# A two-layer graph network: running sums along streams of chunks instead of sums kept by tile

## The chip, the cores and the metric

The kernel runs on one core of a Trainium2 chip (trn2). The metric is the device time of one execution, in microseconds. Engines: TensorE (PE, its weight loads PEld), VectorE (DVE), ScalarE (ACT), GpSimd (POOL) and SyncE (SP), which here only issues DMAs.

## The reference

The graph has N = 1250 nodes, E = 20000 edges (sorted by destination), features of D = 768 floats and 34 relations.

```python
def gatv2(x, src, dst, Ws, bs, Wd, bd, attn):
    fs = (x @ Ws + bs).reshape(-1, H, D)
    fd = (x @ Wd + bd).reshape(-1, H, D)
    e = leaky_relu(fs[src] + fd[dst], 0.2)
    logits = einsum('ehd,hd->eh', e, attn)
    m = segment_max(logits, dst)
    ex = exp(logits - m[dst])
    alpha = ex / segment_sum(ex, dst)[dst]
    return elu(segment_sum(alpha[:, :, None] * fs[src], dst))
h = layer_norm(gatv2(x, ..., attn1) + x)        # 8 heads
h = layer_norm(gatv2(h, ..., attno))            # 1 head
# layer 1: mean over the edges of each (relation, node), 34 products,
# a root product, then a normalised sum over edges
h1 = einsum('rni,rio->no', mean, W_rel) + h @ W_root + b_rgcn
xw = h1 @ W_gcn
out = segment_sum(xw[src] * (dinv[src] * dinv[dst])[:, None], dst) + xw * dinv**2 + b_gcn
```

## The kernel before, in words

Nodes are ranked by their number of incoming edges and stand in ten tiles of 128 partitions. A chunk is four edges (S = 4) of one node; a group is one chunk of each of the 128 nodes of one tile. A tile needs as many groups as its richest node has chunks; a table `tile_of_group` says which tile each group belongs to. For these inputs there are 47 groups; loops run turns of U = 4 groups, so 12 turns, 48 groups. Buffers have four slots, one for each group of a turn.

The stages, in order, with all engines meeting between them:

- First stage: sorting of the edges and the two first projections fs and fd. VectorE builds `tile_of_group` there (lines 714 to 722).
- First attention, 8 heads (`attention`). GpSimd (`gather_edges`, lines 811 to 874) issues four indirect DMAs per group, one row `fs[src]` of 3104 B for each partition (`rows_of`, line 805), and one that reads a group's 4 edge records (line 828); it works out which of them are real (lines 830, 834). Rows are fetched two groups ahead (ROWS_AHEAD = 2), once TensorE has read the slot's old rows. The fd rows of all ten tiles are gathered once (`fdt`, line 1015; nine of the ten behind the first two groups' rows). VectorE and TensorE add fs and fd, ScalarE sums the logits of three edges head by head (line 1038), VectorE does the fourth's, the softmax with a running maximum, and the weighting of three edges (line 1194); TensorE adds the four rows (`pA`, line 1102); VectorE adds this into `acc` of the tile (line 1165).
- Then layer norm and two projections (`settle_first`).
- Second attention, 1 head (`attention_single`, `gather_rows`, lines 910 to 924). For group u, TensorE first runs `add` for group u + 2 (it waits for those rows), then the share products `pA` of group u (16 matmuls, line 1330, which free the slot: `summed`), then the product with the old `acc` (line 1335); ScalarE copies the result back into `acc` (line 1283). VectorE also counts the edges of each relation.
- Then layer norm and the root product (`settle_last`).
- Relation products: per list of 128 (relation, node) pairs, a gather, six transposes, 36 matmuls, a scatter; VectorE cuts the operands in two parts (line 2203 and those behind it).
- Edge sum: GpSimd fetches four rows of the products per group (line 805 again); VectorE works out each edge's weight from the counts by relation (lines 2399 to 2408) and sums two edges of the four, TensorE the other two (`pR`, line 2335), and VectorE adds them to `acc` (line 2383). Beside it a matrix of edge counts between nodes is built (ScalarE line 2304, TensorE `pC`, VectorE line 2375), already transposed.
- The product with W_gcn, then the final product with the count matrix, and the output.

Accumulators (`acc`, `den`, `cntge`, `counts`) live in SBUF by tile; each engine reads the tile number of the turn's groups from `tile_of_group` (`sum_tiles`, line 773). Results are brought from rank order to node order by indirect DMAs.

The order of the work is written out by hand: each engine's instruction list is one queue in order, and GpSimd's indirect DMAs are issued from its own list. What waits at the head of a list holds all behind it.

Of the kernel before, what the change touches and what calls it, by code (L numbers as in the profile page):

```python
# [5 lines left out]
ALU = mybir.AluOpType  # L6
ACT = mybir.ActivationFunctionType
X = mybir.AxisListType.X
# [10 lines left out]
W = D + HEADS  # L19
HALF = D // 2  # L20
# [3 lines left out]
TBACK = 2  # L24
PACK = 6
EROWS = 10016
PROJ_COLS = 100
TG = 5120
# [4 lines left out]
MARKS = 4  # L33
BIG = 1e30
# [35 lines left out]
def gnn_kernel(nc, io, out):  # L70
    ctx = ExitStack()
    with ctx:
# [19 lines left out]
        groups_d = dram("groups_d", (MAX_TURNS * U + U - 1, P, S * 2), I32)  # L92
        by_rank_d = dram("by_rank_d", (NP, 4), I32)
        tile_of_group_d = dram("tile_of_group_d", (TG,), I32)
# [8 lines left out]
        perm_d = dram("perm_d", (NP,), I32)  # L103
# [10 lines left out]
        C_TURNS, C_RANKS, C_PAIRS, C_MORE, C_REL = 0, 2, 3, 4, 8  # L114
        tile_of_group = sb("tile_of_group", [P, TG], I32)
        perm = sb("perm", [P, NT + 1], I32)
        permc = sb("permc", [P, NT + 1], I32)
        degr = sb("degr", [P, NT + 1], F32)
        relbase = sb("relbase", [P, RELS + 1], F32)
        recs = sb("recs", [EP, EC, 2], I32)  # L120
        first_row = sb("first_row", [P, NT + 1], I32)
# [26 lines left out]
        kept_d = dram("kept_d", (P, NT, D), F32)  # L148
# [50 lines left out]

        def w_view(w):  # L200
            return w.rearrange("(c p) n -> p c n", p=P)
# [27 lines left out]
        with stage() as st:  # L229
            lower = sb("lower", [P, P], F32, st)  # L230
            mrow = sb("mrow", [P, 1792], F32, st)
            arow = sb("arow", [P, DA], F32, st)
            gidx = sb("gidx", [P, TG // P, PACK], F32, st)
# [20 lines left out]
            junk = sb("junk", [P, 1792], F32, st)  # L254
# [4 lines left out]
            kmax = sb("kmax", [P, NT], F32, st)  # L259
            kmaxi = sb("kmaxi", [P, NT], I32, st)  # L260
            gend = sb("gend", [P, NT], F32, st)
            small = sb("small", [P, 4], F32, st)
            tog = sb("tog", [P, TG // P, PACK], F32, st)
            packed = sb("packed", [P, TG // P], F32, st)
            togi = sb("togi", [P, TG // P], I32, st)
# [4 lines left out]
             unsorted_sum, deg_sb, deg_out, deg_in, prefixes, ranks, by_rank_out, by_rank_in, maxima, tog_ready,  # L270
             tog_out, tog_in, zero_ready, clear, degr_ready, recs_ready, recs_out, ctl_ok) = sems(
                 st, "const_built", "dve_step", "edges_in", "prev_in", "onehots", "degrees",
                 "backs", "unsorted_sum", "deg_sb", "deg_out", "deg_in", "prefixes", "ranks",
                 "by_rank_out", "by_rank_in", "maxima", "tog_ready", "tog_out", "tog_in",
                 "zero_ready", "clear", "degr_ready", "recs_ready", "recs_out", "ctl_ok")
            CONSTS = 15
# [26 lines left out]
            v_in, dve3, dve3b, copied, posted, none_ok, none_out = sems(  # L303
                st, "v_in", "dve3", "dve3b", "copied", "posted", "none_ok", "none_out")
# [22 lines left out]

            def x_rows(a, i, b, rows, behind=0):
                if isinstance(i, int):
                    at = (2 * i + b) * P + behind  # L330
                    return a[at:at + rows, :]
                return a[ds(i * (2 * P) + (b * P + behind), P), :]

            with nc.Block() as block:
                @block.sync
                def _(sp):
# [22 lines left out]
                    sp.wait_ge(zero_ready, 1)  # L359
                    sp.dma_start(by_dst_d.rearrange("(p f) c -> p (f c)", p=P), zeros[:]).then_inc(clear, 16)  # L360
# [23 lines left out]
                    sp.wait_ge(tog_ready, 1)  # L384
                    sp.dma_start(tile_of_group_d.rearrange("(p c) -> p c", p=P), togi[:]).then_inc(tog_out, 16)
                    sp.wait_ge(tog_out, 16)
                    sp.dma_start(tile_of_group[0:1, :], tile_of_group_d.unsqueeze(0)).then_inc(tog_in, 16)
# [10 lines left out]
                    for s in h_out + f_out[0] + f_out[1]:  # L398
                        sp.wait_ge(s, 16 * 5)
                    sp.wait_ge(none_out, 16)  # L400
                    sp.wait_ge(recs_out, 16)
                    sp.wait_ge(tog_in, 16)

                @block.gpsimd
                def _(pool):
# [2227 lines left out]
```

## Time and profile before

| | us |
|---|---|
| time, three runs | 3326.93, 3327.62, 3331.6 (median 3327.62) |
| span of the profiled execution | 3343.9 |
| first attention, edge loop | about 249 to 907 |
| second attention, edge loop | about 1110 to 1584 |
| relation products | about 1758 to 2741 |
| edge sum | about 2751 to 3140 |
| final product and output | about 3226 to 3344 |

The profile shows one execution; only its span is given for it. "Busy" is the time in which an engine's instructions ran; an arrow names what ended the idle time before an instruction. PEclk is the granted TensorE clock (1.00 is 2.4 GHz, 0.50 is 1.2 GHz).

### The profile page before, as it was taken

To read this page: it belongs to the slowest core of one execution; us is meant where nothing else is said; L and a number is where in the kernel's file an instruction comes from. 1 tells how busy PE (TensorE), PEld (TensorE's weight loads), DVE (VectorE), ACT (ScalarE), POOL (GpSimd) and SP (SyncE) were. 2 spreads that over 40 slices of the span, in tenths; PEclk is the share of its full clock that TensorE was granted. 3 is DMA by queue.
4 is the path that set the end of the run, shared out by engine and by line. 5 is a ranking of instruction groups with operands and counts; after the bars stand their busy time and mean duration, and the time that the engine had idled before them with its cause. 6 is when DMAs were issued, how large, how long until landed. Compare 5 with 4: busy or idle time off the path is not lost. (4 is left out here: it accounts for less than half of the span.)

```text
span 3343.9 us, 59649 instructions
## 1 busy us (share of the span) xinstructions
PE 2854.4 (85%) x13556; PEld 2139.5 (64%) x13557; DVE 2290.3 (68%) x4351; ACT 1702.4 (51%) x5372; POOL 1620.6 (48%) x2067
## 2 busy tenths in 40 slices
PE   5885888888789799998668999999999976777799
PEld 3442454454455455554348999999999974555598
DVE  6535889889767788887565555555555447888743
ACT  0004889899722133332545566555665566777300
POOL 4666566565446555554114545544544445555201
PEclk9897999999999899999789999999999998999899
DMA  4235344444511555555228777777776747666412
GB/s 141 84 81 159 121 135 126 124 134 124 170 46 44 157 167 170 171 170 175 89 95 263 243 242 245 242 237 237 247 241 219 222 144 230 203 210 208 119 34 65
DMA packets 175008, 546.00 MB, mean 163 GB/s; under 512 B 55331, under 2 KB 56343, under 8 KB 174723
## 3 DMA queue, kind: packets, MB, share of 16 engines
q0 software_dynamic: 82000, 370.33, 35.3%
q1 hardware_dynamic: 70596, 122.50, 11.8%
q10 hardware_dynamic: 22304, 52.11, 5.4%
q14 instruction: 86, 0.70, 0.1%
q8 instruction: 22, 0.36, 0.0%
HBM read 461.31 MB, written 83.81 MB: 163 GB/s over the span
## 5 line engine op out<-in xcount | busy, mean ns | idle before, releaser
L2189 PE MATMUL pO<-wh,gT 128*128 128x384 f32 x3264 | 867.1, 339 | 17.6 <-ACT gT L2140 15.6
L805 POOL DMA_INDIRECT row<-fs_d,rec x400 | 455.9, 1140 | 389.6 <-PE pA L1330 157.5
L2189 PEld LDWEIGHTS pO<-wh,gT 128*128 128x128 f32 x3264 | 594.4, 189 | 26.4 <-ACT gT L2140 23.0
L2189 PE MATMUL pO<-wl,gT 128*128 128x384 f32 x1632 | 547.5, 335 | 0.0
L2203 DVE TENSOR_SCALAR cntge<-pT 128x768 int32<-128x768 int32 x137 | 131.2, 958 | 427.2 <-ACT gT L2140 223.1
L1038 ACT ACTIVATE sj<-sj 128x96 f32<-128x96 f32 x1176 | 312.9, 268 | 78.7 <-DVE sj L1155 78.5
L2189 PEld LDWEIGHTS pO<-wl,gT 128*128 128x128 f32 x1632 | 308.3, 189 | 0.0
L2140 ACT ACTIVATE gT<-cntge 128x256 fp32r<-128x256 f32 x822 | 292.9, 410 | 28.1 <-DVE cntge L2206 4.0
L805 POOL DMA_INDIRECT row<-y_d,rec x200 | 204.1, 1020 | 171.6 <-PE pR L2335 113.5
L1077 PE MATMUL pS<-row,ident 128*128 128x384 f32 x400 | 176.2, 524 | 128.3 <-DVE sj L1155 80.9
L2335 PE MATMUL pR<-row,share 128*128 128x384 f32 x384 | 165.7, 582 | 120.6 <-issue 65.0
L170 PE MATMUL pO<-wt,hT 128*128 128x384 f32 (+1 forms) x720 | 242.9, 497 | 19.8 <-issue 8.0
L1330 PE MATMUL pA<-row,share 128*128 128x384 f32 x768 | 255.6, 486 | 1.0 <-ACT share L1296 1.0
L1102 PE MATMUL pA<-row,ident 128*128 128x384 f32 x768 | 255.5, 486 | 0.0
L208 POOL DMA_INDIRECT marked_d<-marks,recc x160 | 201.7, 1261 | 65.4 <-issue 54.2
L2065 POOL DMA_INDIRECT g<-hr_d,gindex x138 | 167.7, 1215 | 121.6 <-POOL keys L2062 60.8
L1038 ACT ACTIVATION_READ_ACCUMULATOR sj<-sj 128x1 f32 x1176 | 220.4, 187 | 0.5 <-issue 0.2
L170 PEld LDWEIGHTS pO<-wt,hT 128*128 128x128 f32 (+1 forms) x720 | 137.7, 193 | 118.6 <-issue 31.5
L1330 PEld LDWEIGHTS pA<-row,share 128*128 128x128 f32 x768 | 145.8, 190 | 103.1 <-issue 1.9
L1102 PEld LDWEIGHTS pA<-row,ident 128*128 128x128 f32 x768 | 145.9, 190 | 101.8
L1077 PEld LDWEIGHTS pS<-row,ident 128*128 128x128 f32 x400 | 76.0, 200 | 202.3 <-DVE sj L1155 109.3
L2129 ACT ACTIVATE acc<-startrow,after 128x1279 bf16<-128x1279 f16 (+1 forms) x139 | 188.1, 1353 | 27.9 <-DMA startrow<-seen_d 27.9
(386 smaller groups left out, 5983.8 us busy)
## 6 DMA issues: line engine op xcount, KB each, us to landing
fdt<-in_L_gnn_W_rel_dram SPq DMA_DIRECT2D x170, 384.0 KB
startrow<-seen_d ACTq DMA_DIRECT2D x141, 320.0 KB
raw<-in_L_gnn_W_rel_dram SPq DMA_DIRECT2D x34, 384.0 KB
row<-fs_d,rec POOLq DMA_INDIRECT x400
kept_d<-fdt SPq DMA_DIRECT2D x10, 384.0 KB
kept<-kept_d SPq DMA_DIRECT2D x10, 384.0 KB
fs_d<-of SPq DMA_DIRECT2D x9, 388.0 KB
fd_d<-of SPq DMA_DIRECT2D x9, 388.0 KB
```

Of the source, the lines that this page charges most:

```text
L170: last = pe.matmul(dst[0:rows, q, 0:HALF], rows_t[:, c * P:c * P + rows], w[:, c, lo:up], start=c == 0, stop=c == KC - 1)
L208: pool.indirect_dma_start(marked_d[k], bass.IndirectOffsetOnAxis(ap=keys, axis=0), marks[0:EP], None)\
L805: pool.indirect_dma_start(b["row"][u][:, j, :].bitcast(words), None, table, bass.IndirectOffsetOnAxis(ap=b["rec"][u][:, 2 * j + field:2 * ...
L1038: last = act.activation(of_head, of_head, ACT.Copy, accum_out=dots[off % U][:, j, h:h + 1])
L1077: pe.matmul(pS[j][:, q, 0:HALF], ident[:], row[off % U][:, S // 2 + j, lo:up], start=True, stop=False)
L1102: last = pe.matmul(pA[:, q, 0:HALF], share, row[u][:, j, lo:up], start=j == 0, stop=j == S - 1)
L1330: last = pe.matmul(pA[u % 2][:, q, 0:HALF], share[u % 2][:, 1 + j, :], row[u][:, j, lo:up], start=j == 0, stop=False)
L2065: pool.indirect_dma_start(g[:, b, :], None, hr_d, bass.IndirectOffsetOnAxis(ap=gindex[b][:], axis=0))\
L2129: act.activation(sign[:, 0:COUNT[b]], seen_row[b][:, 0:COUNT[b]], ACT.Sign, bias=half, scale=-1.0, accum_out=total[b][:]).then_inc(total_o ...
L2140: act.activation(gT[:, c].bitcast(F32R), cut[:, :, c * P:(c + 1) * P], ACT.Copy).then_inc(gT_ok.sem, 1)
L2189: last = pe.matmul(pO[:, q, 0:HALF], gT[:, c, half, :].bitcast(F32R), w[:, c, lo:up].bitcast(F32R), start=c == 0 and k == 0, stop=c == KC ...
L2335: last = pe.matmul(pR[:, q, 0:HALF], share[u % 2][:, k, :], b["row"][u][:, BY_DVE + k, lo:up], start=k == 0, stop=k == S - BY_DVE - 1)
```

## The change

The 1250 nodes are dealt to 128 streams, one for each partition, by rank in turns forward and backward, so that the streams are nearly equally long. A partition walks the chunks of its nine or ten nodes one after another; a group is now the next chunk of every stream. For these inputs the longest stream has 44 chunks: 11 turns, 44 groups, in each of the three edge loops.

Partitions of one group are now at different nodes, so nothing can be kept by tile. Each group reads its own fd row for every partition with a fifth indirect DMA (`own_of`; not in the edge sum); sums run on from group to group in four slots (`sum`), with a flag or a factor `keep` that is zero at a node's first chunk; and each group's running row is scattered to DRAM (`sums_out`, two groups behind), where the rows that are not a node's last lie out of bounds and are skipped. Before a group's record slot is reloaded, GpSimd copies the scatter's target (`keep_target`). In the first attention the fetch of rows (fd row first) stands ahead of the record and of the scatter; in the second attention and in the edge sum the scatter and the copy of the target stand ahead of the fetch.

```diff
+        def keep_target(pool, b, i, off):
+
+            u = off % U
+            sum_free(pool, b, i, off)
+            pool.sem_inc(b["posted"], 1)
+            pool.tensor_copy(b["to"][u][:], word(b, u, R_OUT)).then_inc(b["to_ok"][u], 1)
+        def sums_out(pool, b, i, off, table, done):
+
+            u = off % U
+            for s in done:
+                s.wait(pool, i, off)
+            target_wait(pool, b, i, off)
+            pool.sem_inc(b["posted"], 1)
+            pool.indirect_dma_start(table, bass.IndirectOffsetOnAxis(ap=b["to"][u][:], axis=0), b["sum"][u][:], None,
+                                    bounds_check=NP - 1, oob_is_err=False).then_inc(b["sum_out"][u], 16)
...
+            def fetch(i, off):
+                u = off % U
+                pool.wait_ge(b["edges_only"][u], i * 16 + 16 * (off // U + 1))
+                used.wait(pool, i, off - U)
+                pool.sem_inc(b["posted"], 1)
+                own_of(pool, b, u, own)
+                rows_of(pool, b, u, table, 0, F32)
...
             with pool.Fori(0, turns) as i:
                 for u in range(U):
+                    fetch(i, u + ROWS_AHEAD)
+                    w = u + U - 1
                     rows_wait(pool, b, i, u - 1)
+                    own_wait(pool, b, i, u - 1)
+                    pool.wait_ge(b["saved"][w % U], i * 16 + 16 * (w // U))
+                    pool.wait_ge(b["info_in"][w % U], i * 16 + 16 * (w // U + 1))
                     pool.sem_inc(b["posted"], 1)
+                    record(w % U)
+                    sums_out(pool, b, i, u - LAG, out_table, done)
+                    keep_target(pool, b, i, u)
+                    edges_only(i, w)
+            for k in range(LAG, 0, -1):
+                sums_out(pool, b, turns, -k, out_table, done)
...
+            def fetch(i, off):
+                u = off % U
+                rec_wait(pool, b, i, off)
+                for used in readers:
+                    used.wait(pool, i, off - U)
+                pool.sem_inc(b["posted"], 1)
+                if own is not None:
+                    own_of(pool, b, u, own)
                 rows_of(pool, b, u, table, field, words)
...
                 for u in range(U):
-                    w = u + ROWS_AHEAD
-                    pool.wait_ge(b["rec_in"][w % U], i * 16 + 16 * (w // U + 1))
-                    for used in readers:
-                        used.wait(pool, i, w - U)
-                    pool.sem_inc(b["posted"], 1)
-                    rows_of(pool, b, w % U, table, field, words)
+                    sums_out(pool, b, i, u - LAG, out_table, done)
+                    keep_target(pool, b, i, u)
+                    fetch(i, u + ROWS_AHEAD)
...
+                        def keep(i, off):
+                            whole.wait(act, i, off)
+                            sum_free(act, b, i, off)
+                            act.activation(split(total[off % U][:, 0:D]), halves(pA[off % 2]), ACT.Copy).then_inc(kept.sem, 1)
```

A first-stage loop over blocks of 64 groups writes what each group of each stream needs (16 words: edges or weights, row, node, flags), with 22 steps on VectorE, in place of the ten steps over `tile_of_group`:

```diff
+                    with dve.Fori(0, blocks) as k:
+                        w = Steps(dve, dve_step, k * BLOCK_STEPS + v.base)
+                        w.wait()
+                        w.link(dve.tensor_tensor(begun[:], over(grow[:], 2, shape), over(chunk_from[:], 1, shape), ALU.is_ge))
+                        for f in range(5):
+                            w.link(dve.tensor_tensor(part[:], begun[:], over(rise[:, f, :], 1, shape), ALU.mult))
+                            w.link(dve.tensor_reduce(now[:, f, :], part[:], X, ALU.add))
...
+                        w.mark(dve.scalar_tensor_tensor(out=word(R_OUT), in0=is_last, scalar=float(NP), in1=node,
                                                         op0=ALU.mult, op1=ALU.add))
...
+                        w.mark(dve.tensor_scalar(fword(R_KEEP), is_first, -1.0, 1.0, ALU.mult, ALU.add))
+                        w.mark(dve.tensor_scalar(grow[:], grow[:], float(BLOCK), None, ALU.add))
+                        w.wait()
+                        dve.sem_inc(block_ready, 1)
+                        assert w.n == BLOCK_STEPS, w.n
```

The edge sum takes its weights from these words; they are worked out during the relation products, once for each relation, ahead of the next relation's weights, and the count matrix is kept as running rows of 16-bit integers that are no longer transposed by `pC`:

```diff
+                    def weigh(i, b):
+
+                        v = Steps(dve, weigh_step, i * 6 + (3 * b + 1))
+                        v.wait()
+                        sh = [P, 2 * S, RELS]
+                        at = ds(i * (4 * S) + b * (2 * S), 2 * S) if not isinstance(i, int) else slice((2 * i + b) * 2 * S, (2 * i + b + 1) * 2 * S)
+                        row = ds(i * 4 + b * 2, 2) if not isinstance(i, int) else slice((2 * i + b) * 2, (2 * i + b + 1) * 2)
+                        of_group = crow[:, row, :].unsqueeze(2).to_broadcast([P, 2, S, RELS])
+                        v.link(dve.tensor_tensor(crel[:], over(reld[:, at], 2, sh), over(relid[:], 1, sh), ALU.is_equal))
+                        v.link(dve.tensor_tensor(crel[:].rearrange("p (g s) r -> p g s r", g=2),
+                                                 crel[:].rearrange("p (g s) r -> p g s r", g=2), of_group, ALU.mult))
+                        v.mark(dve.tensor_reduce(cweight[:].rearrange("p g s -> p (g s)")[:, at], crel[:], X, ALU.add))
+                        assert v.n == 3
...
                         cut_rows(end * PAIR, -1)
+                        weigh(i, b)
                         if more:
                             cut_weights(i, b + 1, range(KC // 2))
...
-                            weight_ok.wait(dve, i, u)
+                            compare(i, u + 1)
                             rows_wait(dve, b, i, u)
-                            into = of_acc(tile)
+                            summed.wait(dve, i, u)
+                            used.wait(dve, i, u - 1)
+                            sum_free(dve, b, i, u)
+                            dve.scalar_tensor_tensor(out=split(total[u][:, 0:D]), in0=split(total[(u - 1) % U][:, 0:D]),
+                                                     scalar=word(b, u, R_KEEP, F32), in1=halves(pR),
+                                                     op0=ALU.mult, op1=ALU.add).then_inc(added.sem, 1)
                             for j in range(BY_DVE):
...
+                                dve.scalar_tensor_tensor(out=total[u][:, 0:D], in0=row[u][:, j, :],
+                                                         scalar=word(b, u, R_WEIGHT + j, F32), in1=total[u][:, 0:D],
+                                                         op0=ALU.mult, op1=ALU.add).then_inc(used.sem, 1)
+                            joined.wait(dve, i, u)
+                            counted.wait(dve, i, u - 1)
+                            dve.scalar_tensor_tensor(out=count[u], in0=count[(u - 1) % U], scalar=word(b, u, R_KEEP, F32),
+                                                     in1=pC[u % 2][:].rearrange("p a f -> p (a f)")[:, 0:NP],
+                                                     op0=ALU.mult, op1=ALU.add).then_inc(counted.sem, 1)
```

The later stages load and store plain rows in node order with DMAs of SyncE instead of indirect ones. The product with W_gcn first adds the edge sums that it loads to the root part (ten additions). The final stage loads the counts tile by tile, widens them on VectorE and transposes them on TensorE, ten transposes for each tile:

```diff
+                        def turn(t):
+                            pe.wait_ge(wide_ok, t + 1)
+                            if t > 0:
+                                pe.wait_ge(ch_ok, t)
+                            for c in range(NT):
+                                last = pe.transpose(pW[:, c // 4, (c % 4) * P:(c % 4 + 1) * P], wide[t % 2][:, c * P:(c + 1) * P], ident[:])
+                            last.then_inc(turned, 1)
```

The big memsets of `acc`, the gather of `fdt`, and all reads of `tile_of_group` are gone.

## Rows read from the trace of the kernel before

**Rows 1.** Busy time by engine in five stretches: the three edge loops, root product, last product
```profile
core 0: us, PE busy (x) PEld busy (x) DVE busy (x) ACT busy (x) POOL busy (x), PEclk, DMA share, GB/s
300.00:907.00 607.00, 523.08 (x1546) 295.00 (x1544) 538.52 (x1002) 541.75 (x3124) 359.62 (x472) 0.98 0.44 131
1130.00:1584.00 454.00, 439.36 (x1337) 251.90 (x1336) 383.78 (x1047) 136.54 (x345) 233.40 (x184) 1.00 0.58 170
1587.00:1758.00 171.00, 114.06 (x332) 61.54 (x332) 101.51 (x203) 83.21 (x106) 26.04 (x51) 0.80 0.29 97
2760.00:3140.00 380.00, 274.22 (x2304) 194.16 (x2304) 324.10 (x532) 275.52 (x288) 201.04 (x197) 0.90 0.67 206
3226.00:3344.00 118.00, 106.14 (x600) 105.82 (x600) 43.26 (x42) 0.00 (x0) 12.30 (x10) 0.95 0.22 70
```

**Rows 2.** First attention, VectorE: the line run once for each group
```profile
L1165 DVE TENSOR_TENSOR acc<-pA,scaled x49: 946/947/958, 306.6 to 905.1; 128x768 f32 x49
```

**Rows 3.** First attention, VectorE timeline: the first instruction of two groups, start and length
```profile
...
613.40 0.19 DVE L1175 TENSOR_TENSOR lg<-dots,lin 128x32 f32<-128x32 f32 x1 [0.73 <-ACT sj L1038]
...
625.46 0.22 DVE L1175 TENSOR_TENSOR lg<-dots,lin 128x32 f32<-128x32 f32 x1
```

**Rows 4.** First attention, GpSimd timeline of its first groups
```profile
...
290.26 0.95 POOL L1015 DMA_INDIRECT fdt<-fd_d,permc  x1 [0.30 <-issue]
...
300.99 0.20 POOL L825 COPY now<-left 128x2 f32 x1
...
309.58 1.43 POOL L805 DMA_INDIRECT row<-fs_d,rec  x1 [0.30 <-issue]
```

**Rows 5.** First attention, GpSimd by line: busy us, mean ns, idle before
```profile
L805 POOL DMA_INDIRECT row<-fs_d,rec x182 | 186.7, 1026 | 165.9 <-PE pA L1102 111.5 <-issue 42.0 <-POOL rec L834 12.4
```

**Rows 6.** First attention, TensorE's share sums: durations, first and last start
```profile
L1102 PE MATMUL pA<-row,ident x768: 486/486/486, 309.9 to 904.3; 128*128 128x384 f32 x192
```

**Rows 7.** Second attention, ScalarE: the line run once for each group
```profile
L1283 ACT ACTIVATE acc<-pA x49: 784/810/813, 1130.8 to 1582.7; 128x768 f32 x49
```

**Rows 8.** Second attention, timeline of one group and the fetch behind it
```profile
...
1300.20 5.32 PE L1330 MATMUL pA<-row,share 128*128 128x384 f32 x16
...
1305.36 1.45 PE L1335 MATMUL pA<-acc,share 128*128 x4
1306.34 1.41 POOL L805 DMA_INDIRECT row<-fs_d,rec  x1 [3.44 <-PE pA L1330]
...
1307.08 0.81 ACT L1283 ACTIVATE acc<-pA 128x768 f32 x1 [2.15 <-PE pA L1335]
...
1311.12 0.95 POOL L805 DMA_INDIRECT row<-fs_d,rec  x1 [0.30 <-issue]
...
1315.88 0.91 PE L1312 MATMUL pS<-row,ident 128*128 128x384 f32 x2
```

**Rows 9.** Second attention, waits: us in total, times, longest
```profile
PE pS L1312 <- DMA row<-fs_d,rec: 7.4, 13, 1.2
```

**Rows 10.** Second attention, GpSimd by line
```profile
L805 POOL DMA_INDIRECT row<-fs_d,rec x182 | 231.5, 1272 | 192.5 <-PE pA L1330 149.5 <-issue 43.0
```

**Rows 11.** The whole span, GpSimd by line: a scatter of full rows
```profile
L1761 POOL DMA_INDIRECT hr_d<-ht,sindex x10 | 9.8, 979 | 35.2 <-ACT ht L1805 35.2
```

**Rows 12.** Edge sum, VectorE: the line run once for each group
```profile
L2383 DVE TENSOR_TENSOR acc<-acc,pR x49: 933/942/955, 2767.4 to 3136.2; 128x768 f32 x49
```

**Rows 13.** Edge sum, GpSimd by line
```profile
L805 POOL DMA_INDIRECT row<-y_d,rec x190 | 194.5, 1024 | 164.4 <-PE pR L2335 113.5 <-issue 45.4 <-DVE acc L2421 4.6
```

**Rows 14.** First stage, VectorE timeline
```profile
...
109.15 5.00 DVE L716 SCALAR_TENSOR_TENSOR tog<-gidx,gend,tog 128x240 f32<-128x240 f32 x10
```

**Rows 15.** First stage, TensorE timeline
```profile
...
119.95 0.88 PE L163 MATMUL pT<-ident,ht 128*128 128x128 f32 x6
...
137.67 2.92 PE L170 MATMUL pO<-wt,hT 128*128 128x384 f32 x4 [4.78 <-DVEq L754]
```

**Rows 16.** Relation products, VectorE by line
```profile
L2203 DVE TENSOR_SCALAR cntge<-pT 128x768 int32<-128x768 int32 x137 | 131.2, 958 | 427.2 <-ACT gT L2140 223.1 <-PE pT L163 203.2 <-issue 0.9
```

More of the change, by code:

```diff
@@ L23 @@
 U = 4
-TBACK = 2
-PACK = 6
 EROWS = 10016
 PROJ_COLS = 100
-TG = 5120
+BLOCK = 64
+GROUPS = 5120
+WORDS = 16
+R_ROW, R_NODE, R_LEFT, R_FLAG, R_OUT, R_KEEP, R_NODEF = range(8, 15)
+R_WEIGHT = S * 2
 MAX_TURNS = (E // S + NT) // U + 1
@@ L832, in edges_only @@
-            def edges_only(u):
-                pool.tensor_tensor(b["rec"][u][:], b["rec"][u][:], b["edge"][u][:], ALU.mult).then_inc(b["edges_only"][u], 16)
-            ahead = sum_tiles(pool, 0, U - 1, 0)
-            for u in range(U - 1):
-                record(pre, u, ahead[u])
-                pre.wait()
-            for u in range(ROWS_AHEAD):
-                pool.wait_ge(b["rec_in"][u], 16)
-                edges_only(u)
-                pool.wait_ge(b["edges_only"][u], 16)
-                rows_of(pool, b, u, table, 0, F32)
@@ new lines, in fetch @@
+            def fetch(i, off):
+                u = off % U
+                pool.wait_ge(b["edges_only"][u], i * 16 + 16 * (off // U + 1))
+                used.wait(pool, i, off - U)
+                pool.sem_inc(b["posted"], 1)
+                own_of(pool, b, u, own)
+                rows_of(pool, b, u, table, 0, F32)
+            for u in range(U - 1):
+                pool.wait_ge(b["info_in"][u], 16)
+                record(u)
+            for off in range(ROWS_AHEAD):
+                edges_only(0, off)
+                fetch(0, off)
@@ L996, in attention @@
                 lin_ok = Signal(st, "lin_ok", 1, U, U)
-                top_ok = Signal(st, "top_ok", 1, U, U)
                 den_ok = Signal(st, "den_ok", 1, U, U)
-                row = b["row"]
-                def fdt_row(tile):
-                    return fdt[:, tile, :] if isinstance(tile, int) else fdt[:, ds(tile, 1), :].rearrange("p o f -> p (o f)")
+                row, own, total = b["row"], b["own"], b["sum"]
                 with nc.Block() as block:
@@ L1100, in _ @@
                                     for q, lo, up in HB:
-                                        share = ident[:] if heads > 1 else shares[:, j, :]
-                                        last = pe.matmul(pA[:, q, 0:HALF], share, row[u][:, j, lo:up],
+                                        last = pe.matmul(pA[:, q, 0:HALF], ident[:], row[u][:, j, lo:up],
                                                          start=j == 0, stop=j == S - 1)
@@ L2378, in add @@
-                    def add(i, off, tile):
-                        summed.wait(dve, i, off)
-                        used.wait(dve, i, off)
-                        into = split(of_acc(tile))
-                        dve.tensor_tensor(into, into, halves(pR), ALU.add).then_inc(added.sem, 1)
+                    for u in range(U - LAG, U):
+                        pre.mark(dve.memset(total[u][:], 0.0))
+                    dve.wait_ge(node_ok, 1)
+                    pre.link(dve.tensor_copy(of_node[:], node[:]))
```

1114 lines of the change are left out of this document (590 added, 524 removed).

## The prediction

> **What bounds the kernel now.** I read the busy time by stretch first, then in each edge loop the line that runs once per group, then the timeline of one group. Three loops take 1441 of the 3343.9 us of span, and no engine is the bound in all of them. First attention [rows 1]: VectorE 539 and ScalarE 542 us busy of 607. 48 intervals of line 1165 take 905.1 - 306.6 = 598.5 us [rows 2], so 12.47 us a group; inside a turn two groups stand 12.06 apart [rows 3], and the rest is lost at turn boundaries. Second attention: TensorE 439 of 454 us at full clock; 48 intervals of line 1283 take 451.9 us [rows 7], 9.41 a group. Edge sum: VectorE 324 of 380, 48 intervals in 368.8 us [rows 12], 7.68 a group. In the last product TensorE works 106 of 118 us.
>
> The reader should see a second limit in the second attention [rows 8]. TensorE's sums of a group end at 1305.52; that frees a row slot; GpSimd's four fetches start at 1306.34 and the last at 1311.12; the matmul that needs them starts at 1315.88, 4.8 after that, and in 13 of the 46 groups it is seen waiting for its rows, by up to 1.2 [rows 9]. Then come 2.7 us of `pS` (8 half matmuls at 5.32/16 = 0.33) and 5.32 of `pA`, which free the next slot but one: 10.36 + 2.7 + 5.3 = 18.4 us for two groups, 9.2 for one. The loop from a slot's release to its next release is as long as TensorE's own work. Whatever is put into it is paid in full, half of it per group.
>
> **The change part by part.** From the inputs the longest stream has 44 chunks, where the tiles needed 47: 44 groups instead of 48 in each loop. Everything else is price.
>
> *First attention.* VectorE does about the same per group (a copy goes, the running sum is written to a new slot) but reads no tile numbers at turn boundaries: 12.0. GpSimd gets more. Its unhindered turn of one group is now 309.58 + 1.43 - 300.99 = 10.0 us [rows 4]. Three small operations and their hand-overs go (-1.5), the own fd row comes (0.95 to 1.03 + 0.30 = 1.3 [rows 5]), the scatter (0.98 + 0.30 [rows 11]), the copy of the target (0.4) and a little waiting for the record that it has just asked for and now masks at once, not one group later: 11.5, and with the slower GpSimd operations that stand beside VectorE up to 13. Nothing hides it, but it is not in a short loop: rows are asked for two groups ahead. Two engines at nearly 12.0 give 12.3 (bounds 11.8 and 13.1): 44 x 12.3 = 541, minus 598.5 = -57. At the start, nine fd gathers (1.25 each, until 291.2 [rows 4]) stood between the second group's rows and the third's, and the first share sum waited for those until 309.9 [rows 6]; they go, with the large memset, against two fd rows and masks in order: -20. At the end the last scatter has to land: +3. Sum -74 (-95 to -30).
>
> *Second attention.* The scatter waits for the sum of its group to be copied by ScalarE, and stands ahead of the fetch. From the slot's release: 1.3 to the end of the old sum's product, 0.3 and 0.8 for ScalarE's copy (ends 1307.89 [rows 8]), 0.8 until GpSimd starts (as at 1306.34), 0.98 for the scatter [rows 11], 0.6 for the copy of the target and the hand-over, 0.3, then the own fd row, 1.27 + 0.30 [rows 10]: the first row is asked for 6.6 us after the release, now 0.8. That is +5.8 (5.2 if the fd row takes 0.95). Behind it nothing changes. 18.4 + 5.8 = 24.2 for two groups, 12.1 for one; with GpSimd's operations quicker beside a less busy VectorE (0.95 against 1.27 on average, five of them) 11.3. I take 11.85, nearer to the upper end since the sample group's fetches were themselves under the mean: 44 x 11.85 = 521, minus 452 = +69. The fill is +3 (two fd rows), the last scatter +5. Sum +77. Bounds: if the loop did not bind, 44 x 9.41 = 414 and -38 + 8 = -30; with 12.6, +110.
>
> *Edge sum.* VectorE loses the four operations that make weights; at 324/48 = 6.75 now it falls to about 6.3. GpSimd: five indirect DMAs of 1.02 [rows 13] with 0.30 between them, the copy of the target and two hand-overs, 7.3 (7.0 if all are quick, 8.0 if each hand-over takes 0.8). Here the release of a slot and its next use lie four groups apart, so the order scatter-then-fetch costs nothing but the engine's time. 44 x 7.3 = 321, minus 369 = -48; start -3 (no zeroing of the counts), last scatter +4. Sum -47 (-65 to -10).
>
> *The rest.* First stage: ten steps over 240 elements (5.00 us [rows 14]) and seven small ones, 7.4 in all, give way to a block with eleven steps over 640 elements, by their size 0.8 each, and eleven small ones: 13 to 14. TensorE waits for VectorE there [rows 15], so +6 (+3 to +10). Layer norm after the first attention: plain loads of the same rows, +2. Root product: 48 small gathers on GpSimd, which is busy 26 of 171 us [rows 1], hide; the chain of relation counts moves ahead of the sums: +3 (-5 to +11). Relation products: 34 times three VectorE operations over 272 elements, some 1.2 us each time; VectorE stands idle 427 us ahead of its first cut alone [rows 16], but at a change of relation they come before the new weights: +3 (0 to +20). Product with W_gcn: the ten additions hide behind TensorE except the first, +3. Last product: 100 transposes of 0.88/6 = 0.147 us [rows 15] on the engine that is the bound, 14.7, and a first widening; one output DMA less on GpSimd's way: +15. Sum +32.
>
> Total: -74 + 77 - 47 + 32 = -12 us. This is worked against the profiled execution, 3343.9 us of span, 16.3 us (0.5%) above the median; scaling changes nothing that counts. 3327.6 - 12 = 3316.
>
> Scatters of which most rows are dropped do not occur in the trace before. The nearest is a scatter of full rows at 0.98 [rows 11]; skipped rows may make it cheaper (0.5) or the bound test dearer (2). In the second attention 0.5 less is -11, 1 more is +22; in the edge sum as much times two. I take 0.98 and keep the ends for the range.
>
> **A rule weighed.** In the second attention TensorE works 97% of the time and the granted clock is 1.00; in the edge sum it works 72% with gaps for which it waits and the granted clock is 0.90 [rows 1]. After the change the second attention has TensorE busy 9.1 of 11.85 us, 77%, with one long wait for rows in each group. The Trainium skill, "TensorE: Matmul & The Clock Gate", section "HAM oscillation — how this bites in real kernels", describes a kernel whose matmuls are shorter than its waits for data and which therefore falls back to the lower clock every time. By that rule the wait would also slow the matmuls; by the clock of 1.00 it would not, and my sum has it so. The trace agrees as far as the edge sum shows.
>
> **The rivals.**
>
> 1. *The loop does not bind* (something in my chain runs beside the rest). Second attention -30 instead of +77: 3209. Against it: the 13 waits for rows in the loop before, and that each link is an order written in the code. Chance 0.08.
>
> 2. *The clock falls in the second attention* (the other side). 9.4 us of matmuls (1.45 + 2.7 + 5.3) lie in the loop over two groups. At the edge sum's 0.90 they take 1.0 more, 0.5 per group, +23; at the root product's 0.80 [rows 1] 2.35, 1.2 per group, +52. In the middle +37: 3353. It decides as soon as a group takes over 12.3. For it: 23% of waiting. Against: the first attention, with 14% of waiting, keeps 0.98. Chance 0.22.
>
> 3. *GpSimd is the bound and slow*: 13.0 per group in the first attention (+31), 7.8 in the edge sum (+22), since each of its operations is exposed to VectorE's: 3369. For it: 1.27 us per fetch in the second attention against 1.03 in the first [rows 5, 10]. Against: with GpSimd as the bound, VectorE has pauses in which it runs free. Chance 0.14. [...]
>
> 4. *The trade is better than I think*: first attention at 11.9 per group and scatters at 0.5 us: -18 - 11 - 21 = -50, 3266. It lies in my range's lower part. For it: most rows of a scatter are skipped. Against: so far a scatter costs what a fetch does [rows 11]. Chance 0.10.
>
> **How the numbers follow.** The forecast, 3316 (its own range 3290 to 3340), has 0.46; the rivals 0.08, 0.22, 0.14 and 0.10. Below 3250 lies rival 1, above 3380 a tail of rivals 2 and 3; the range is 3250 to 3380. A measurement of this kernel tells 0.2% (6.7 us) from no change. Faster (below 3321): 0.6 of the forecast's 0.46, rivals 1 and 4, little of 2: 0.47. Same (3321 to 3334): 0.22 of 0.46 and 0.05: 0.15. Slower: 0.38.
>
> **What would show it.** In the changed kernel's trace: 45 executions of the per-group lines; 12.3 us a group in the first attention, 11.85 in the second with GpSimd's scatter ahead of the fetch and TensorE waiting for rows about 2.5 us in every group at clock 1.00; 7.3 in the edge sum with GpSimd busy or handing over all the time; a first share sum some 40 us after the start of the first attention, not 60. I am wrong if the second attention takes under 10.5 a group (rival 1), if its clock is 0.90 or less (rival 2), or if GpSimd's own turn in the other loops is over 12.8 or 7.7 us (rival 3).

## The result and the profile after

The changed kernel takes 3429.34 us (median of 4 runs, 3421.63 to 3433.7) against 3329.61 for the kernel before (median of 4, 3326.93 to 3334.01): slower, ratio 1.0295, 95% interval 1.028 to 1.0309. The forecast was 3316 in a range of 3250 to 3380. The profiled execution of the changed kernel has a span of 3419.9 us.

Each line that runs once per group, in the three edge loops of the changed kernel (durations, first and last start); they answer to [rows 2], [rows 7] and, with one execution less since it counts in the same turn, [rows 12]:

```profile
L1261 DVE TENSOR_TENSOR sum<-pA,scaled x45: 946/957/959, 292.2 to 879.6; 128x768 f32<-128x768 f32 x45
L1365 ACT ACTIVATE sum<-pA x45: 787/810/811, 1112.8 to 1681.9; 128x768 f32<-128x768 f32 x45
L2522 DVE SCALAR_TENSOR_TENSOR sum<-sum,rec,pC x44: 1534/1543/1543, 2878.9 to 3188.9; 128x1280 int16<-128x1280 int16 x44
```

So a group takes 587.4/44 = 13.35 us in the first attention (12.47 before, 12.3 forecast), 569.1/44 = 12.93 in the second (9.41, 11.85), and 310.0/43 = 7.21 in the edge sum (7.68, 7.3). The two attentions by engine (columns as in [rows 1]):

```profile
300.00:880.00 580.00, 487.50 (x1392) 274.75 (x1390) 480.59 (x853) 488.02 (x2796) 405.55 (x427) 0.94 0.52 159
1130.00:1682.00 552.00, 439.63 (x1206) 248.99 (x1204) 339.86 (x873) 118.86 (x306) 301.23 (x295) 0.90 0.54 166
```

In the second attention no engine is busy for even 80% of the time, and the clock has fallen from 1.00 to 0.90. Laid out by milestones, the two profiled executions differ by 76 us of span:

| stretch | change forecast | measured |
|---|---|---|
| start to the first attention's first sum | -14 | -14.4 |
| first attention, 44 intervals against 48 | -57 | -11.1 |
| to the second attention's first copy | +8 | +7.5 |
| second attention, 44 against 48 | +69 | +117.2 |
| to the first relation product | +8 | +14.7 |
| relation products | +3 | -16.1 |
| to the last count of the edge sum | -51 | -47.0 |
| to the first product with W_gcn | +7 | +14.8 |
| the last two products and the output | +15 | +10.6 |

The medians differ by 100, not 76, because the profiled execution of the kernel before was 14 us above its median and that of the changed kernel 9 below. One stretch that varies between executions is the relation products: in the profiles of the changed kernel and of the eleven variants below, none of which touches them, they take 959 to 974 us, against 975 in the one profile of the kernel before. Of the -16, most is therefore not put down to the change; a few us may belong to it.

One group of the second attention in the changed kernel, its timeline (start us, us):

```profile
...
1307.07 1.45 PE L1414 MATMUL pA<-sum,share 128*128 128x384 f32 x4
...
1308.36 0.81 PE L1393 MATMUL pS<-row,ident 128*128 128x384 f32 x2
...
1308.63 0.81 ACT L1365 ACTIVATE sum<-pA 128x768 f32<-128x768 f32 x1 [13.22 <-PE pA L1414]
...
1310.47 1.65 POOL L896 DMA_INDIRECT second_d<-sum,to  x1 [6.82 <-issue]
...
1310.94 5.32 PE L1409 MATMUL pA<-row,share 128*128 128x384 f32 x16
...
1312.11 0.93 POOL L887 COPY to<-rec 128x1 int32<-128x1 int32 x1
...
1313.20 1.01 POOL L847 DMA_INDIRECT own<-fd_d,rec  x1 [0.16 <-issue]
...
1318.26 0.95 POOL L843 DMA_INDIRECT row<-fs_d,rec  x1 [0.30 <-issue]
...
1323.61 1.64 PE L1393 MATMUL pS<-row,ident 128*128 128x384 f32 x2 [6.06 <-DMA row<-fs_d,rec]
...
1328.64 1.78 PE L1409 MATMUL pA<-row,share 128*128 128x384 f32 x5
```

This is the chain the prediction laid out, link by link: end of the sum, ScalarE's copy, scatter, copy of the target, fd row, four rows, the wait, `pS`. The reader should see three links that are longer in this group than I had them: the scatter 1.65 (I had 0.98), the last request to its use 5.35 (4.8), and `pS`, which needs 5.0 us (1323.61 to 1328.64) and not 2.7, since it runs at the lower clock just after TensorE stood idle for 6.06 (granted clock 0.50 from 1323.6 to 1328.2).

The groups come in pairs. `pS` of one group starts right behind the sum of the group before and takes 2.6 us (1308.36 to 1310.94, granted clock 1.00); `pS` of the next waits for its rows and is slow. From 1130 to 1682, 22 groups are of the first kind, with `pS` at 2.58 on average, and 21 of the second, with a wait of 5.3 (112.2 us in all) and `pS` at 4.78, between 4.1 and 5.3. The forecast had the same waiting spread evenly, 2.5 in every group.

GpSimd in the first attention of the changed kernel, by line (busy us, mean ns, idle before; window 300 to 870, 43 groups):

```profile
L843 POOL DMA_INDIRECT row<-fs_d,rec x169 | 196.6, 1163 | 51.7 <-issue 51.7
L847 POOL DMA_INDIRECT own<-fd_d,rec x42 | 50.4, 1199 | 42.2 <-POOL rec L922 29.9 <-issue 10.7 <-PE pA L1197 1.5
L896 POOL DMA_INDIRECT first_d<-sum,to x44 | 47.4, 1077 | 14.1 <-issue 14.1
L909 POOL DMA_INDIRECT rec<-by_dst_d,rec x43 | 41.9, 974 | 13.1 <-issue 13.1
L918 POOL TENSOR_SCALAR edge<-slot,rec 128x8 int32<-128x8 f32 x43 | 37.0, 861 | 35.4 <-issue 35.2
L887 POOL COPY to<-rec 128x1 int32<-128x1 int32 x43 | 18.6, 433 | 0.0
L922 POOL TENSOR_TENSOR rec<-rec,edge 128x8 int32<-128x8 int32 x43 | 14.6, 340 | 8.0 <-POOL edge L918 8.0
```

Busy 406.5 and idle 164.5 make 571 us, the whole window, and of the idle time only 1.5 us ends on another engine (`pA`). The rest is GpSimd handing over to itself or, by my reading of the 35.2 us before the mask (L918), waiting for the record that it has just asked for: in e3 and e5 below, which ask for it earlier, the mask waits 0.0 and 1.0 us in all. 571/43 = 13.3: the period of the loop is GpSimd's list.

### The profile page after: what moved, and what is told of

Same layout as the page of the kernel before. It is cut to its first block and busy times, and to the rows that moved or that the text cites. A ratio compares the mean times of both kernels' runs of the same rounds, so it can differ in the third digit from the quotient of the medians.

```text
span 3419.9 us, 54141 instructions
## 1 busy us (share of the span) xinstructions
PE 2814.0 (82%) x11992; PEld 2066.6 (60%) x11993; DVE 2190.5 (64%) x3987; ACT 1615.7 (47%) x5047; POOL 1773.2 (52%) x2181
## 5 line engine op out<-in xcount | busy, mean ns | idle before, releaser
L843 POOL DMA_INDIRECT row<-fs_d,rec x368 | 421.4, 1145 | 112.4 <-issue 111.5
L2328 DVE TENSOR_SCALAR cut<-pT 128x768 int32<-128x768 int32 x137 | 131.0, 956 | 362.0 <-ACT gT L2263 186.5
L1138 ACT ACTIVATE sj<-sj 128x96 f32<-128x96 f32 x1080 | 287.4, 267 | 76.9 <-DVE sj L1250 76.8
L2263 ACT ACTIVATE gT<-cut 128x256 fp32r<-128x256 f32 x822 | 291.4, 410 | 27.5 <-DVE cut L2331 4.3
L1176 PE MATMUL pS<-row,ident 128*128 128x384 f32 x368 | 172.5, 554 | 127.5 <-DMA row<-fs_d,rec 126.1
L1365 ACT ACTIVATE sum<-pA 128x768 f32<-128x768 f32 x45 | 36.4, 810 | 441.3 <-PE pA L1414 441.3
L1441 DVE TENSOR_TENSOR leak<-row,own 128x768 f32<-128x768 f32 x135 | 121.3, 954 | 182.8 <-DMA row<-fs_d,rec 182.8
L1409 PE MATMUL pA<-row,share 128*128 128x384 f32 x704 | 235.6, 488 | 0.0
L1197 PE MATMUL pA<-row,ident 128*128 128x384 f32 x704 | 234.2, 486 | 0.0
L1393 PE MATMUL pS<-row,ident 128*128 128x384 f32 x184 | 104.8, 661 | 139.1 <-DMA row<-fs_d,rec 139.1
L2252 ACT ACTIVATE sign<-startrow,after 128x1279 bf16<-128x1279 f16 (+1 forms) x139 | 188.4, 1356 | 28.5 <-DMA startrow<-seen_d 26.1
```

Of the source, the lines that this page charges most:

```text
L843: pool.indirect_dma_start(b["row"][u][:, j, :].bitcast(words), None, table, bass.IndirectOffsetOnAxis(ap=b["rec"][u][:, 2 * j + field:2 * ...
L1138: last = act.activation(of_head, of_head, ACT.Copy, accum_out=dots[off % U][:, j, h:h + 1])
L1176: pe.matmul(pS[j][:, q, 0:HALF], ident[:], row[off % U][:, S // 2 + j, lo:up], start=True, stop=False)
L1197: last = pe.matmul(pA[:, q, 0:HALF], ident[:], row[u][:, j, lo:up], start=j == 0, stop=j == S - 1)
L1409: last = pe.matmul(pA[u % 2][:, q, 0:HALF], share[u % 2][:, 1 + j, :], row[u][:, j, lo:up], start=j == 0, stop=False)
L2252: act.activation(sign[:, 0:COUNT[b]], seen_row[b][:, 0:COUNT[b]], ACT.Sign, bias=half, scale=-1.0, accum_out=total[b][:]).then_inc(total_o ...
```

## The experiments

All are variants of the changed kernel (3429 us), timed against the kernel before in turns on the same chip. "Period" is the spacing of the per-group lines above.

**e1 and e2: fetch ahead of the scatter.**

```diff
                 for u in range(U):
+                    fetch(i, u + ROWS_AHEAD)
                     sums_out(pool, b, i, u - LAG, out_table, done)
                     keep_target(pool, b, i, u)
-                    fetch(i, u + ROWS_AHEAD)
```

e1 in both stages that use this loop, e2 in the second attention alone.

> The changed kernel (3429 us, 12.93 us a group in the second attention, 7.2 in the edge sum) with the fetch of rows put ahead of the scatter and the copy of the target in both the second attention and the edge sum. Theory: the second attention is set by a loop over two groups (release of a slot, sum, copy, scatter, copy of the target, fetch, landing, sums); the order alone put about 5.8 us into it. Without it 18.4 + 1.6 for the own fd row and about 1 for a longer burst = 21 us for two groups, or GpSimd's own 9.7 us: 9.9 to 10.5 a group, 44 x -2.7 = -120; the edge sum is bound by GpSimd's total and stays at 7.2; the last fetches go out sooner, so each stage drains up to 5 us sooner. 3290 to 3315 us. Rival: the order costs nothing and the second attention is slow for its fifth DMA, its traffic and its clock: 3420 to 3430.

> Fetch ahead of the scatter in the second attention only; the edge sum keeps the scatter first. Theory: nearly all of the gain of the kernel with both, since the edge sum's slot comes back only after four groups: within 8 us of it, so 3295 to 3320. Rival: the edge sum's order costs as much per group as the second attention's: 50 us or more above the kernel with both.

Measured: e1 3330.27 us, ratio to the kernel before 0.9995 (0.9982 to 1.0009); e2 3327.53, 0.9985 (0.9976 to 0.9995). The line of e1:

```profile
L1365 ACT ACTIVATE sum<-pA x45: 785/811/814, 1116.3 to 1579.8; 128x768 f32<-128x768 f32 x45
```

463.5/44 = 10.53 us a group, at a clock of 0.99. The order alone is worth 44 x 2.4 = 106 us in this stage, as much as the 99 by which the change is slower. Some 0.95 of the 2.4 is the clock: its waits for rows are shorter (1.6 us on average, 28 of them from 1130 to 1575), and `pS` takes 2.73 on average, against (4.78 + 2.58)/2 = 3.68. The times miss the upper bounds of 3315 and 3320 by 15 and 8 us. A group gained 2.4 and not 2.7, which is 13 us, and the stage does not drain sooner, as the theory had it: from the last copy to the first instruction of the next stage it is 13.0 us in e1 (1579.8 to 1592.8) and 13.5 in the changed kernel (1681.9 to 1695.4). In the edge sum the period is 7.13 with fetch first and 7.15 with scatter first: there the order is free, as predicted.

**e9: the scatter three groups behind**, still ahead of the fetch.

```diff
-        LAG = 2
+        LAG = 3
```

> The changed kernel with one constant changed: sums are scattered three groups behind instead of two (in all three loops), the scatter still ahead of the fetch. Theory: what the second attention pays for is the wait of the scatter for a sum that was only just finished; three groups behind, the scatter and the copy of the target run before the slot is released, and the order is harmless: 10.3 to 11.0 a group, like fetch-first (10.53), 3325 to 3345 us. Rival: it is the GpSimd time in front of the fetch (scatter 1.2, copy 0.4, hand-overs) that costs, wait or no wait: 1.6 to 2.4 us stay in the loop of two groups, 11.4 to 12.0 a group, 3360 to 3395 us. First attention and edge sum: no change.

Measured: 3334.0 us, 1.0016 (1.0001 to 1.0031), period 10.51 in the second attention (45 executions of L1365, first and last start at 1120.6 and 1583.2). In the first attention the period is 13.50, as in e10, which leaves that stage alone, and in the edge sum 7.12: no change, as expected.

So it is not GpSimd's time for the scatter that costs. It is that the scatter, at the head of the list, waits for a sum which is finished only after the slot is released, and holds the fetch behind it. When the sum is one group older, scatter and copy run while GpSimd has nothing to do.

**e7: no fd row in the second attention.** The fd rows are a constant there, so that part of the computation is left out.

```diff
-                    own_of(pool, b, u, own)
+                    pool.sem_inc(b["own_in"][u], 16)
```

> The changed kernel without the fifth DMA of the second attention: the fd rows are a constant there (so this part of the computation is left out), the scatter stays ahead of the fetch. Theory of the loop over two groups: 1.3 to 1.4 us go from a chain of 25.9, and up to 1.5 of the transfer, which was a quarter longer: 12.93 down to 11.5 to 12.3 a group, -28 to -63: 3366 to 3401 us. Rival (GpSimd's total is the bound, 9.3 us of it): a full 1.4 per group, and rival (the scatter alone is the cause): under 10 us in all, above 3419.

Measured: 3383.63 us, 1.0158 (1.0129 to 1.0186), 46 us below the changed kernel; period 11.95, clock 0.93. One DMA of 1.09 + 0.30 us less takes 0.98 from the period, a good two thirds of it. Half, 0.70, is its place in a chain of two groups. A further 0.31 is the clock: after its wait `pS` takes 4.15 on average here, against 4.78. Together that is 1.01. A loop bound by GpSimd's total would give 1.4.

**e3, e4 and e5: GpSimd's list in the first attention.** e4 puts the fd row behind the four rows. e3 asks for the next record ahead of the fetch; e5 also copies the target there:

```diff
                 for u in range(U):
-                    fetch(i, u + ROWS_AHEAD)
                     w = u + U - 1
...
                     record(w % U)
+                    keep_target(pool, b, i, u)      # e5 only
+                    fetch(i, u + ROWS_AHEAD)
                     sums_out(pool, b, i, u - LAG, out_table, done)
-                    keep_target(pool, b, i, u)      # e5 only
                     edges_only(i, w)
```

> The changed kernel with one thing moved in the first attention: GpSimd asks for the next edge records before it fetches rows, not after, so that they have landed when it masks them. Theory: GpSimd's own list is the bound there (13.35 us a group = four rows 4.65 + fd row 1.2 + record 0.97 + scatter 1.08 + copy and masks 1.6 + hand-overs and waits 3.8); 0.8 us of waiting for the record and some of the 0.9 before the fetch go: 12.0 to 12.6 a group, 44 times -0.75 to -1.35 = -33 to -60: 3370 to 3396 us. Rival: the loop is bound by the transfers of the rows (TensorE waits for them 92 us there): no change, 3422 to 3436.

> The changed kernel with the fd row fetched after the four source rows in the first attention instead of before. Theory (GpSimd's list is the bound): the same operations in the same list, no change beyond 0.2%: 3422 to 3436. Rival: the fd row is what VectorE and TensorE wait for first, and last in the list it lands 1.3 us x 4 later for the first addition: up to +0.5 us a group, 3440 to 3451.

> As e3 (record asked for ahead of the fetch in the first attention), and the copy of the scatter's target also ahead of the fetch, so that SyncE's load of the next record words, which waits for that copy, is done a group earlier. Base: the changed kernel, 3429 us. Theory: GpSimd's own list is the bound; e3 failed because its record request then waited 2.8 us for that load. Now neither wait is left: per group five fetches 7.2, record 1.3, scatter 1.4, copy and masks 1.5, hand-overs 0.6: 12.0 to 12.5 instead of 13.35, -37 to -60: 3369 to 3392 us. Rival (the rows' transfers are the bound): 3422 to 3445.

Measured: e4 3431.04 us, 1.0312 (1.029 to 1.0334), period 13.35, no change: the fd row's place, first or last, does nothing. e3 3445.52, 1.0353 (1.0333 to 1.0373), period 13.61: worse, against both theories. Its waits (total, times, longest) say why:

```profile
POOL rec L909 <- DMA rec<-groups_d: 100.4, 37, 3.8
```

The record's request needs words that SyncE loads only once GpSimd has copied the slot's old target, and that copy now stood only 3.7 us ahead of the request (586.92 and 590.60 in one group), which waited 2.8 us for the load. I moved an operation past its queue and did not ask what else it waits for. e5 moves the copy too: 3377.2 us, 1.0146 (1.0113 to 1.0179), 52 below the changed kernel:

```profile
L1261 DVE TENSOR_TENSOR sum<-pA,scaled x45: 945/948/958, 293.5 to 829.4; 128x768 f32<-128x768 f32 x45
```

12.18 a group instead of 13.35. The same transfers and the same number of operations on every engine, but GpSimd's list (window 300 to 820) holds 9.2 us of work and 2.95 of idle time per group instead of 9.45 and 3.83: GpSimd was the bound.

**e10: a memset of 768 floats per group in the edge sum's list.**

> The changed kernel with a memset of 768 floats, which no one needs, put into GpSimd's list of the edge sum, once per group ahead of the fetch. Theory: GpSimd's list is the bound there (7.2 us a group); the memset (0.73 us for 768 in this kernel's trace, 0.2 of hand-over) is paid in full: +0.9 to 1.0 a group, +37 to +46: 3466 to 3475 us. Rival (VectorE, ScalarE or the transfers at 240 GB/s are the bound): less than +15, below 3444 us.

Measured: 3485.61 us, 1.0464 (1.0437 to 1.0491), 56 more than the changed kernel and 10 above the expected range. GpSimd by line in the edge sum (window 2900 to 3200):

```profile
L843 POOL DMA_INDIRECT row<-y_d,rec x142 | 147.9, 1041 | 64.5 <-issue 29.9 <-POOL spare L1031 26.4 <-DVE sum L2522 6.4
```

The memset takes 0.79 (28.3 us in 36) and the fetch waits 26.4/36 = 0.73 for it, not 0.2: 1.5 us, of which 1.12 arrive in the period (8.33 against 7.21). The missing 0.4 is no slack: the first row no longer has its own hand-over of some 0.3, and rows take 1.04 on average against 1.09. Without the memset the list is already full, with 248.1 us busy and 58.6 idle in the 305 from 2880 to 3185, and under 7 of these idle us end on another engine or on a load of SyncE. The edge sum is bound by GpSimd.

**e8: twelve turns instead of eleven.**

```diff
-  small[:, 0:1], most[:], float(U - 1), None, ALU.add
+  small[:, 0:1], most[:], float(2 * U - 1), None, ALU.add
```

> The changed kernel with twelve turns forced instead of eleven: four empty groups more in each of the three loops, as many groups as the kernel before. This isolates what the better packing is worth. By the periods measured: 4 x (13.35 + 12.93 + 7.2) = 134 us: 3550 to 3570. If empty groups (all partitions at the same dummy row) run faster than real ones: 3520 to 3550.

Measured: 3564.1 us, 1.0701 (1.067 to 1.0732), 135 more. The better packing is worth 135 us at this kernel's own periods. The change lost more than that on the price of each group: 44 x (13.35 - 12.47 + 12.93 - 9.41 + 7.21 - 7.68) = 173 us.

**e6 and e11: what the experiments point to.** e6 is e1 with e5; e11 adds the third group of e9.

> e1 (fetch first in the second attention and the edge sum) with e5 in the first attention. If both theories hold the gains add: 3330 - 37 to 60 = 3270 to 3293 us, faster than the kernel before. If only e1's holds: 3323 to 3340.

> e6 (3273 us) with the scatter three groups behind. Theory: fetch-first has already taken the scatter out of the loop, so nothing is left to gain: 3266 to 3280 us. Rival: sums that wait for their scatter to be done (a slot is rewritten two groups after it is sent) now stall, one group less of room: 3285 us and more.

Measured: e6 3273.04 us, ratio 0.9823 (0.9794 to 0.9852), faster than both kernels (1.8% below the kernel before); its periods are 12.20, 10.43 and 7.09. The two gains add (99 + 52 = 151; 156 measured). e11 is 3279.76, 0.9846 (0.9826 to 0.9867): nothing gained in the second attention (10.49), 0.5 us a group lost in the first (12.70), 0.2 gained in the edge sum (6.87), so how far behind to scatter is a choice for each stage.

## Why the prediction was wrong

*The second attention, +69 forecast, +117 measured.* The mechanism was right: slot release, sum, copy, scatter, fetch, landing and sums form a loop over two groups, and e1 and e9 show it. The step that failed is the term `pS`, 2.7 us at a granted clock of 1.00, which stood in the sum although the wait before it was in the sum too. The links of the loop, as worked out and as the mean of its 21 turns from 1130 to 1682 of the changed kernel's trace:

| link (us) | worked out | measured |
|---|---|---|
| old sum's product, until ScalarE's copy starts | 1.6 | 1.50 |
| ScalarE's copy | 0.8 | 0.81 |
| until GpSimd starts | 0.8 | 0.99 |
| scatter | 0.98 | 1.31 |
| copy of the target and hand-over | 0.9 | 0.80 |
| fd row and hand-over | 1.57 | 1.47 |
| first row request to the last | 4.78 | 3.80 |
| last request to its use | 4.8 | 5.13 |
| `pS` | 2.7 | 4.78 |
| `pA` | 5.3 | 5.22 |
| two groups | 24.2 | 25.8 |

25.8 for two groups is the period, 12.9. I had gone from 12.1 down to 11.85, on the hope that GpSimd's fetches would get quicker. They did (-1.1 in the loop; 1.13 on average against 1.27 in [rows 10]); the scatter (+0.3) and the landing (+0.4) took most of it back. What is left of the miss is `pS`: 4.78 against 2.7, 1.04 a group or 46 us in the stage, nearly all of 117 - 69. My second rival had this cause, but priced the clock of 0.90 at half, +0.5 per group. It spread the lower clock evenly over the 18 us of matmuls of two groups, of which 9.4 lie in the loop. In the trace the slow matmuls are those that follow the wait, and they all lie in the loop: two groups hold 18.1 us of matmuls at the full clock, the slow ones add 2.1, and 18.1/(18.1 + 2.1) = 0.90 is the clock of the whole stage. The clock of the stage is 0.90 with TensorE idle 20% of the time and 0.99 in e1 with 9%. The rule of the Trainium skill that I weighed ("TensorE: Matmul & The Clock Gate", section "HAM oscillation — how this bites in real kernels": in its example the waits for data bring the lower clock back each time) comes out as the trace shows it, behind all 21 waits, although the matmuls between two waits here take some 20 us and are not shorter than the wait of 5.3. It belonged in the sum.

*The first attention, -57 forecast, -11 measured.* The step that failed is the period of 12.3, "two engines at nearly 12.0". GpSimd's list was not at 12.0 but at 13.3. I had its items but took them from a group in which nothing disturbed it ([rows 4]); in the loop a row costs 1.16, a mask 0.86 and a copy 0.43. The wait for the record, "a little" in the prediction, is 35.2/43 = 0.8 for each group, and the hand-over from the mask to the fetch 0.7 more (29.9/43). So the term was mis-sized, 11.5 to 12.0 for a list that takes 13.3; that GpSimd's list is the bound, e5 shows. My third rival had 13.0.

So rival 2 and the half of rival 3 that concerns the first attention came true together (in the edge sum the period is 7.21, not 7.8). I had treated them as alternatives, each with its own time (3353 and 3369), and ended the range at 3380 because each alone was below it. They are independent (in e6 the two gains add), they concern different stages, and their prices add: 3316 + 37 + 31 = 3384 already lies outside. That is the error in the range.

*The packing.* Right: four groups less in each loop, and e8 puts 135 us on them.

*The edge sum, -51 with its fill, -47 measured:* right, and for the reason given (e10). *The start of the first attention and the first stage, -14 forecast, -14.4 measured:* two misses that cancel, so luck. The first attention starts 1.5 us later (248.7 before, 250.2 after; +6 forecast), and its first sum comes 16.0 sooner after that start (57.9 before, 42.0 after; -20 forecast). The first share sum stands 49.5 us behind the start, where I had some 40. *Transposes and the last products, +15:* +10.6. *The relation weights in idle VectorE time, +3:* nothing of them is seen in the length of that stage.

*The ends of the stages.* I gave the last scatters +3, +5 and +4. In the changed kernel GpSimd's last scatter of the second attention and the first instruction of the next stage:

```profile
1683.65 1.01 POOL L896 DMA_INDIRECT second_d<-sum,to  x1 [7.95 <-ACT sum L1365]
1695.37 0.12 POOL L1847 MEMSET under<- 34x34 f32 x1 [10.71 <-POOLq L152]
```

10.7 us of nothing. The trace of the kernel before had this price, at the end of its relation products, and I did not look for it:

```profile
2742.74 0.99 POOL L2075 DMA_INDIRECT y_d<-fdt,kindex  x1 [0.80 <-POOL kindex L2074]
2751.40 0.21 POOL L2287 MEMSET zero<- 128x128 f32 x1 [7.67 <-POOLq L144]
```

From the last copy or sum of a loop to the next stage's first instruction it was 1.9, 1.9 and 2.5 us in the kernel before, where the loops did not end in a scatter, and is 10.6, 13.5 and 12.2 in the changed kernel. That is +8.6, +11.6 and +9.8 where I had +3, +5 and +4, and it makes most of the +14.7 and +14.8 of the table where I had +8 and +7. That the row with +7.5 is met (+8) is luck: the layer norm stage took +0.8 (+2 forecast) and the fill of the second attention -1.9 (+3).

*Rival 1 (the loop does not bind)* is excluded by e1 and e9. *Rival 4 (cheap scatters)* is excluded: scatters of which most rows are skipped took 1.07 to 1.17 us of GpSimd on average, as much as the scatters of full rows in the relation products of the same trace (1.06 and 1.17), and the first attention is at 13.35.

## What to carry to other kernels

On an engine whose list is one queue, ask of each instruction at its head when its own input is ready, not how long it takes: the same scatter costs nothing one group later (e9) and 2.4 us per group where it waits. Before moving a request forward, follow all that it waits for, through the other queues too: e3 lost what e5 won because a load on another queue hung on the copy left behind. Where a chain makes TensorE wait, price its next matmuls in the chain at the lower clock, and not all of its matmuls at the stage's mean. And add up the rivals: if two of them concern different stages, the range has to hold their sum.

## What the runs showed of the hardware

- After the last scatter of a stage, 7.1 to 10.7 us pass until the next stage's first instruction (7.1 behind the layer norm stage of the kernel before), also where the data queues are idle: in e1 the scatter is issued at 1581.47, the transfers are over by 1584 and the next stage starts at 1592.8. What fills this time none of the runs shows.
- In a steady loop TensorE's clock can fall and rise once per turn: in the second attention of the changed kernel `pS` takes 4.78 us on average behind each of 21 waits for rows of 5.3 us on average, and 2.58 in each of the 22 groups between, which start without a wait.
- GpSimd's small operations vary by a factor of six beside a busy VectorE (the mask of 128 x 8 takes 0.30 to 1.83 us in the changed kernel, 0.86 on average in the loop), and the same operation averages 0.36 in e5, where it stands behind the scatter, whose own mean rises there from 1.08 to 1.54. Prices for GpSimd have to come from the means of the loop, not from one clean group. The Trainium skill ("SBUF — State Buffer", section "Who interferes with whom") names an exclusive port lock between VectorE and GpSimd; the spread fits such a lock, but no run here takes VectorE's operations away to show it.
